# A selective-scan kernel: the scan in half blocks of channels, state sums in two column halves, the first residual on TensorE and ScalarE, and a new order of slots and transfers

## The chip, the cores and the metric

One core of one Trainium2 chip runs the whole kernel in one launch. The time is device microseconds of that core; the traces come from one profiled execution.

## The reference

For each of 64 batch entries `h` is a (205, 1024) float32 matrix: 128 rows of a token mixer (a long convolution kernel computed from `x`) and 77 rows of text. Then come a selective scan and a feed-forward layer, each on a layer norm and each added back:

```python
h = concatenate([tok(x), txt], axis=1)             # 64 x 205 x 1024
h = h + attn(layernorm(h))                         # the scan, below
h = h + ffn(layernorm(h))                          # 1024 x 1024 weights from a 4-bit table
# attn(x): dt_in (32), B (16), C (16) = x @ x_proj_w.T ; dt = softplus(dt_in @ dt_proj_w.T + b)
# per channel d (1024) and state n (16), over the 205 rows t:
#   s[t] = exp(dt[t] * A[d, n]) * s[t-1] + dt[t] * B[t, n] * x[t]
#   y[t] = sum over n of s[t] * C[t, n]   + D[d] * x[t]
```

Rows whose norm is over 64 would take 8-bit weights; a count at the end of the kernel decides that, and with these inputs none does.

## The kernel before

Three stages come first: constants, the token mixer (written to a DRAM tensor `mixed`) and the dense weights `w_low`. `scan_pass` then works through the 64 entries and takes most of the time. It is software pipelined: while entry u is scanned, entry u+1 is prepared (norm, transpose, projections, `dt`, `u = dt * x`), entry u-1 is continued (first residual `add`, second norm, first half of the feed-forward layer) and entry u-2 is ended (`ffn_late`, `out_low`, `out_high`).

**Chunks.** Channels lie on partitions: block j (0 to 7) holds 128 channels. An entry is 32 chunks; chunk s is block s//4 with four of its 16 states, 4 x 205 = 820 columns. For each chunk:

- ScalarE (ACT) writes the four decays `exp(dt * A)` into one of two PSUM buffers (L1003), once the chunk two before has been done with its buffer.
- GpSimd (POOL) writes `u * B` into a slot of `ring` with 8 slots (L1107).
- VectorE (DVE) scans (L1162) and, for the chunks in `ON_DVE` (19 of 32), multiplies by C (L1168). For the other 13 POOL multiplies by C, three chunks later (L1113).
- TensorE (PE) sums the four states, `LAG` = 3 chunks later: four float32 matmuls of the identity by 205 columns of the ring slot, accumulated in `y_ps` (L899), behind one with a diagonal of D at the start of a block (L893). After a block's last chunk ACT copies `y_ps` back into `x_t` (`blk`, L1041), and PE may start the next block.

**Order.** Each engine runs 32 slots to an entry. Slot s does the engine's part of chunk s and then what its plan (`PE_PLAN`, `ACT_PLAN`, `DVE_PLAN`, `POOL_PLAN`) lists for s. The plans are constants of the file. Everything that crosses between PE and another engine goes through two PSUM banks `xch`, in the order of `X_ORDER`, taken in turn. Entries -1 to 2 and the last three are unrolled; the others run in a hardware loop with two entries to an iteration, one such loop for each engine.

**First residual.** PE transposes `x_t` into `xch` (L915), DVE adds it to the rows in `h1` (`add`, L1183), ACT then sums the 1024 columns for the mean (`mean2`, L1019, L1022).

**Reset.** One scan instruction covers four states; `reset` (L1085) adds 1e37 to `dt` at time 0 of each block, so that the decay is 0 there.

**Transfers.** SP issues all DMAs of an entry in a fixed order and waits in it: `keep` (h1 to DRAM after the last `add`), `load` (rows of entry u+2 into `x_in`), `spread` (B and C rows to DRAM and back, broadcast over 128 partitions, into `bc`), `write` (out), `load_rows` (rows of entry u into `h1`): 10 DMAs.

Of the kernel before, what the change touches and what calls it, by code (L numbers as in the profile page):

```python
# [13 lines left out]
F32 = mybir.dt.float32  # L14
# [6 lines left out]
P = 128  # L21
# [22 lines left out]
CHUNKS = ND * NS // CN  # L44
# [18 lines left out]
def constants(nc, t, dram, kept):  # L63

    with ExitStack() as ctx:
# [10 lines left out]
        vec = sb("c_vec", [2 * ND, P])  # L76
        ps = [ctx.enter_context(nc.psum_tensor(f"c_ps{i}", [P, 512], F32)) for i in range(4)]
# [7 lines left out]
        def _(sp):  # L85
            sp.dma_start(t["a_neg"][:, :, :], dram["A_log"].rearrange("(j p) n -> p j n", p=P)).then_inc(alog_in, 16)
# [52 lines left out]
        def _(dve):  # L139
# [7 lines left out]
            for c0 in range(0, P, 32):  # L147
# [11 lines left out]
            link(dve, dve_step, n, nc.vector.tensor_scalar(  # L159
                t["a_neg"][:, :, :], t["a_neg"][:, :, :], -1.0, A_MOST, ALU.mult, ALU.min))  # L160
# [332 lines left out]
def dense_weights(nc, t, dram):  # L493
# [3 lines left out]
    with ExitStack() as ctx:  # L497
# [98 lines left out]
        def _(pe):  # L596
# [964 lines left out]
```

## Time and profile before

| | |
|---|---|
| median of 3 runs | 6199.3 us (6199.27 to 6200.41) |
| profiled execution: its own time | 6200.29 us |
| profiled execution: span of the core | 6198.4 us |
| mean granted TensorE clock | 0.979 |
| busy PE, DVE, ACT, POOL over the span | 93%, 92%, 83%, 92% |
| POOL's first instruction of scan entry 0 | at 503.63 us |

The busy shares are over all stages; the entries of the scan are read one by one, from one first POOL instruction of an entry to the next.

### The profile page before, as it was taken

Reading aid. Unit: us, or ns where it says so; the run is one execution under the profiler, and the core shown is the slowest. Engines: PE = TensorE matmul, PEld = TensorE weight load, DVE = VectorE, ACT = ScalarE, POOL = GpSimd, SP = SyncE. Lnnn points to the kernel's source line nnn. Section 1 sums busy time; section 2 is a strip of 40 time slices with the busy share of each in tenths; the row PEclk is TensorE's granted clock in tenths of the full one; section 3 lists DMA queues with packets and bytes.
Section 4 is the critical chain, followed back from the end, with each engine's and each line's share of the span. In section 5 each row is a group of like instructions: output and inputs, shape, how many; then the busy total and the mean of one; then the engine's idle time right before and its main releaser. Section 6 shows DMA issues by size and latency. Waiting matters only on the chain. (4 is left out here: it accounts for less than half of the span.)

```text
span 6198.4 us, 111922 instructions
## 1 busy us (share of the span) xinstructions
PE 5792.6 (93%) x35091; PEld 5385.1 (87%) x35091; DVE 5699.7 (92%) x4564; ACT 5122.6 (83%) x12831; POOL 5709.3 (92%) x3484
## 2 busy tenths in 40 slices
PE   4686999999999999999999999999999999999998
PEld 3555899999999999999999999999999999999997
DVE  8766999999999999999999999999999999999996
ACT  5716888888888888888888888888888888888885
POOL 4627999999999999999999999999999999999995
PEclk9887999999999999999999999999999999999999
DMA  4701222122212221222122212221222212221220
GB/s 94 161 2 66 83 88 71 67 83 88 74 64 83 88 78 66 78 88 83 61 78 88 88 56 80 86 88 61 77 83 88 72 67 83 88 78 61 83 83 34
DMA packets 115881, 478.49 MB, mean 77 GB/s; under 512 B 17441, under 2 KB 52401, under 8 KB 107122
## 3 DMA queue, kind: packets, MB, share of 16 engines
q1 hardware_dynamic: 115314, 471.10, 22.2%
q8 instruction: 335, 5.49, 0.4%
q14 instruction: 232, 1.90, 0.1%
HBM read 327.82 MB, written 143.24 MB: 76 GB/s over the span
## 5 line engine op out<-in xcount | busy, mean ns | idle before, releaser
L1107 POOL TENSOR_TENSOR s_ring<-s_bc,s_u_t 128x820 f32<-128x820 f32 x2048 | 3617.5, 1788 | 4.2 <-DMA s_bc<-rows_bc 4.2
L1003 ACT ACTIVATE s_decay<-s_dt_t,a_neg 128x205 f32<-128x205 f32 x8192 | 3047.2, 420 | 418.4 <-DVE s_ring L1168 347.5
L899 PE MATMUL s_y_ps<-s_ring,ident 128*128 128x205 f32 x16384 | 3140.6, 341 | 113.5 <-issue 61.5
L899 PEld LDWEIGHTS s_y_ps<-s_ring,ident 128*128 128x128 f32 x16384 | 2864.1, 191 | 204.9 <-POOL s_ring L1113 112.8
L1162 DVE TENSOR_TENSOR_SCAN s_decay<-s_decay,s_ring 128x820 f32<-128x820 f32 x1216 | 2265.0, 1863 | 193.6 <-ACT s_decay L1003 180.0
L1113 POOL TENSOR_TENSOR s_ring<-s_ring,s_bc 128x820 f32<-128x820 f32 x832 | 1605.4, 1930 | 77.7 <-DVE s_ring L1162 77.6
L1162 DVE TENSOR_TENSOR_SCAN s_ring<-s_decay,s_ring 128x820 f32<-128x820 f32 x832 | 1543.3, 1855 | 40.9 <-ACT s_decay L1003 40.9
L932 PE MATMUL s_xch<-s_x_t,w_low 128*128 128x205 f32 x8192 | 1523.6, 338 | 0.6 <-ACT s_x_t L1046 0.2
L932 PEld LDWEIGHTS s_xch<-s_x_t,w_low 128*128 128x128 f32 x8192 | 1422.0, 190 | 35.4 <-issue 30.6
L1168 DVE TENSOR_TENSOR s_ring<-s_decay,s_bc 128x820 f32<-128x820 f32 x1216 | 1230.2, 1012 | 41.7
L893 PE MATMUL s_y_ps<-s_x_t,s_d_diag 128*128 128x205 f32 x1024 | 279.6, 355 | 35.1 <-ACT s_x_t L1041 35.1
L1046 ACT ACTIVATE s_x_t<-s_xch 128x512 f32<-128x512 f32 (+1 forms) x512 | 244.5, 502 | 66.0 <-PE s_xch L923 64.4
L1128 POOL TENSOR_TENSOR s_u_t<-s_dt_t,s_x_t 128x410 f32<-128x410 f32 x256 | 271.7, 1061 | 18.1 <-DVE s_dt_t L1190 18.1
L1060 ACT ACTIVATE s_y_t<-s_xch,y_bias 128x205 f32<-128x205 f32 x512 | 213.7, 417 | 89.8 <-PE s_xch L932 89.8
L1041 ACT ACTIVATE s_x_t<-s_y_ps 128x205 f32<-128x205 f32 x512 | 169.6, 331 | 140.9 <-PE s_y_ps L899 140.3
L964 PE MATMUL s_p_ps<-s_xp,dtw_t 33*128 33x205 f32 x1024 | 248.2, 363 | 7.6 <-DVE s_dt_t L1190 7.1
L437 PE MATMUL t_kb<-t_mag,t_gw 128*128 128x256 f32 x512 | 138.8, 431 | 104.5 <-POOL t_gw L319 104.5
L893 PEld LDWEIGHTS s_y_ps<-s_x_t,s_d_diag 128*128 128x128 f32 x1024 | 169.7, 190 | 75.7 <-ACT s_x_t L1041 57.9
L964 PEld LDWEIGHTS s_p_ps<-s_xp,dtw_t 33*128 33x128 f32 x1024 | 166.2, 188 | 66.4 <-issue 56.9
L437 PEld LDWEIGHTS t_kb<-t_mag,t_gw 128*128 128x128 f32 x512 | 106.6, 215 | 127.1 <-POOL t_gw L319 62.6
L1197 DVE TENSOR_TENSOR s_h<-s_xch,s_h 128x512 f32<-128x512 f32 (+1 forms) x256 | 172.6, 675 | 37.6 <-PE s_xch L946 37.6
L955 PE MATMUL s_p_ps<-s_x_t,xpw_t 128*65 128x205 f32 x1024 | 200.8, 339 | 0.6 <-ACT s_x_t L1046 0.6
(165 smaller groups left out, 4224.0 us busy)
## 6 DMA issues: line engine op xcount, KB each, us to landing
s_bc<-rows_bc SPq DMA_DIRECT2D x64, 3280.0 KB, 11.0
mixed<-t_res SPq DMA_DIRECT2D x32, 1024.0 KB, 9.5
s_x_in<-mixed SPq DMA_DIRECT2D x64, 512.0 KB
s_h<-mixed SPq DMA_DIRECT2D x64, 512.0 KB
before<-s_h SPq DMA_DIRECT2D x64, 512.0 KB
out<-s_h SPq DMA_DIRECT2D x64, 512.0 KB
s_x_in<-in_txt SPq DMA_DIRECT2D x64, 308.0 KB
s_h<-in_txt SPq DMA_DIRECT2D x64, 308.0 KB
```

The costliest lines, as they stand in the source:

```text
L437: last = nc.tensor.matmul(kb[b][:, QL * k:QL * k + QL], gw[:, half, h, 2 * k:2 * k + 2, :], mag[:, half, h * QL:(h + 1) * QL], start=True, ...
L893: nc.tensor.matmul(y_ps, d_diag[:, j, :], x_t[:, par, j, :], start=True, stop=False)
L899: last = nc.tensor.matmul(y_ps, ident[:, :], ring[:, c % RING, n * LEN:(n + 1) * LEN], start=False, stop=(c % 4 == 3 and n == CN - 1))
L932: last = nc.tensor.matmul(bank[:, 0:LEN], t["w_low"][:, i, P * o:P * o + P], x2_t[:, i, :], start=(i == 0), stop=(i == ND - 1))
L964: last = nc.tensor.matmul(p_ps[:, LEN * k:LEN * k + LEN], t["dtw_t"][:, P * j:P * j + P], xp[0:RANK + 1, :], start=True, stop=True)
L1003: last = A.activation(decay[s % 2][:, n * LEN:(n + 1) * LEN], dt_t[:, par, j, :], ACT.Exp, scale=t["a_neg"][:, j, n0 + n:n0 + n + 1])
L1046: A.activation(target[:, 4 * side:4 * side + 4, cols(k)], bank[:, 0:4 * w].rearrange("p (j l) -> p j l", j=4), ACT.Copy).then_inc(empty, 1)
L1107: nc.gpsimd.tensor_tensor(ring[:, s % RING, :].rearrange("p (n l) -> p n l", n=CN), bc[:, par, n0:n0 + CN, :], u_t[:, j, :].unsqueeze(1).b ...
L1113: nc.gpsimd.tensor_tensor(ring[:, c % RING, :], ring[:, c % RING, :], bc[:, par, n0:n0 + CN, :].rearrange("p n l -> p (n l)"), ALU.mult).t ...
L1128: nc.gpsimd.tensor_tensor(u_t[:, 2 * r:2 * r + 2, :], dt_t[:, par, 2 * r:2 * r + 2, :], x_t[:, par, 2 * r:2 * r + 2, :], ALU.mult).then_in ...
L1162: V.tensor_tensor_scan(out=decay[s % 2] if s in ON_DVE else ring[:, s % RING, :], data0=decay[s % 2], data1=ring[:, s % RING, :], initial= ...
L1168: V.tensor_tensor(ring[:, s % RING, :], decay[s % 2], bc[:, par, n0:n0 + CN, :].rearrange("p n l -> p (n l)"), ALU.mult).then_inc(dve_hc, 1)
```

## The change

- **Half blocks.** A half block is 64 channels; its even states lie on partitions 0 to 63 and its odd states on 64 to 127. An entry is 16 half blocks (`NB`) x 8 states on a partition (`NK`) / 4 = 32 chunks of 820 columns, as before. `dt` and `u` are computed in the old layout (`dt_n`, `u_n`) and copied into the new one (`dt_t`, `u_t`) by DMAs within SBUF, four for each pair of blocks: 32 more DMAs an entry. `bc` holds 16 rows on a partition instead of 32 and comes in two DMAs.
- **Column-half sums.** A sum now also folds partition halves: the stationary is `stack` (two 64 x 64 identities, one above the other, 128 x 64), the output a 64-partition half of `y_ps`. Two chunks are summed together, matmul by matmul in turn: chunk c into the lower half, c+1 into the upper. The product with D becomes two matmuls of 64 columns' width. PE sums in even slots, `SUM_LAG` = 4.
- **First residual.** PE multiplies the identity by the rows in `h1` (512 columns, float32) and accumulates the transposes as ordinary matmuls on top; ACT copies the bank to `h1` and takes the row sum of each half on the way. DVE's `add` and the two long passes of `mean2` go; two short ones stand in `mean2`.
- **Reset.** Time 0 of `dt_t` is set once, and the copies leave it out; `reset` goes.
- `ON_DVE` has 20 chunks instead of 19; POOL multiplies 12.
- The plans, `X_ORDER` and the order of SP (`SP_ORDER`) are new. `load` and `load_rows` now come behind the copy of `u` for the next entry.

```diff
-CHUNKS = ND * NS // CN
+NB, NK = 2 * ND, NS // 2
+CHUNKS = NB * NK // CN
-PE_PLAN = {1: [("ffn_late", 4)], 2: [("add", 0), ("add", 1)], 6: [("add", 2), ("ffn_late", 5)], 7: [("out_low", 0)],
...
+PE_PLAN = {1: [("ffn_late", 4)], 3: [("ffn_late", 5)], 4: [("add", 0), ("out_low", 0)], 5: [("add", 1), ("add", 2)],
+           6: [("ffn_late", 6)], 7: [("add", 3)], 8: [("turn1", 0), ("ffn_late", 7)], 9: [("turn1", 1)], 10: [("turn1", 2)],
+           11: [("out_high", 0)], 13: [("turn1", 3)], 14: [("xproj", (0, 4)), ("xproj", (4, 8))], 15: [("out_high", 1)],
+           18: [("dt", 0)], 19: [("out_low", 1), ("turn2", 0), ("turn2", 1), ("dt", 1)], 20: [("turn2", 2), ("turn2", 3)],
+           22: [("ffn", 0), ("dt", 2)], 24: [("ffn", 1)], 26: [("ffn", 2)], 28: [("dt", 3)], 31: [("ffn", 3)]}
+ACT_PLAN = {0: [("mean1", 0)], 1: [("var1", 0), ("ffn_late", 4)], 2: [("blk", -1)], 3: [("ffn_late", 5), ("mean1", 1)],
+            4: [("add", 0), ("var1", 1)], 5: [("add", 1)], 6: [("norm1", 0)], 7: [("add", 2)], 8: [("blk", 0), ("ffn_late", 6)],
+            9: [("norm1", 1), ("add", 3)], 10: [("mean2", 0)], 11: [("mean2", 1), ("turn1", 0)],
...
+DVE_PLAN = {3: [("out_low", 0)], 12: [("out_high", 0)], 15: [("out_high", 1)], 18: [("out_low", 1)], 19: [("dt", 0)],
+            22: [("dt", 1)], 27: [("dt", 2)], 31: [("dt", 3)]}
+POOL_PLAN = {4: [("u_hi", 2)], 6: [("root1", 0)], 8: [("u_hi", 3)], 17: [("root2", 0)], 24: [("u_lo", 0)], 31: [("u_lo", 1)]}
+SP_ORDER = [("u_hi", 2), ("u_hi", 3), ("keep", 0), ("spread", 0), ("steps", 0), ("write", 0), ("u_lo", 0), ("load", 0),
+            ("load_rows", 0), ("steps", 1), ("steps", 2), ("u_lo", 1), ("steps", 3)]
-ON_DVE = (1, 3, 4, 5, 7, 9, 11, 13, 14, 15, 17, 19, 21, 23, 24, 25, 27, 29, 31)
+ON_DVE = (1, 3, 4, 6, 8, 9, 10, 12, 13, 14, 15, 17, 20, 21, 25, 26, 27, 29, 30, 31)
+            def halves(target, place, source, r, first, signal):
+                for i in range(2):
+                    for h in range(2):
+                        sp.dma_start(target[64 * i:64 * i + 64, place + h:place + 4:2, first:],
+                                     source[64 * h:64 * h + 64, 2 * r:2 * r + 2, first:]).then_inc(signal, 16)
+            def steps(v, par, r):
+                wait(sp, p_empty, v * P_USES + r + 2)
+                halves(dt_t, dt_place(par, 4 * r), dt_n, r, 1, dt_in[r])
+            def inputs(v, r):
+                wait(sp, u_done, v * 4 + r + 1)
+                halves(u_t, 4 * r, u_n, r, 0, u_in[r])
-                    nc.tensor.matmul(y_ps, d_diag[:, j, :], x_t[:, par, j, :], start=True, stop=False)
+                    for h in range(2):
+                        nc.tensor.matmul(y_ps[sides[h], :], d_diag[:, j, sides[h]], x_t[:, par, j, :], start=True, stop=False)
                 for n in range(CN):
-                    last = nc.tensor.matmul(y_ps, ident[:, :], ring[:, c % RING, n * LEN:(n + 1) * LEN],
-                                            start=False, stop=(c % 4 == 3 and n == CN - 1))
-                last.then_inc(sum_done, 1)
+                    for h in range(2):
+                        last = nc.tensor.matmul(y_ps[sides[h], :], t["stack"][:, :], ring[:, (c + h) % RING, n * LEN:(n + 1) * LEN],
+                                                start=False, stop=(c % 4 == 2 and n == CN - 1))
+                        if n == CN - 1:
+                            last.then_inc(sum_done, 1)
             def chunk(u, par, s, x, scan, after):
-                if s >= LAG and scan:
-                    sums(u, par, s - LAG)
+                if s % 2 != SUM_SLOT:
+                    return
+                if s >= SUM_LAG and scan:
+                    sums(u, par, s - SUM_LAG)
             def add(v, par, r, x):                                     # PE
+                nc.tensor.matmul(bank[0:rows(k), :], ident[0:rows(k), 0:rows(k)], h1[0:rows(k), par, k, 512 * side:512 * side + 512],
+                                 start=True, stop=False)
                 for j in range(4):
-                    last = nc.tensor.transpose(bank[0:rows(k), P * j:P * j + P], x_t[:, par, 4 * side + j, cols(k)], ident[:, :])
+                    last = nc.tensor.matmul(bank[0:rows(k), P * j:P * j + P], x_t[:, par, 4 * side + j, cols(k)], ident[:, :], start=False, stop=(j == 3))
+            def add(v, par, r, x):                                     # ACT
+                A.activation(h1[0:rows(k), par, k, 512 * side:512 * side + 512], bank[0:rows(k), :], ACT.Copy,
+                             accum_out=half_sum[0:rows(k), k, side:side + 1]).then_inc(empty, 1)
```

## Rows read from the trace of the kernel before

**Rows 1.** The page: busy time, share of the span and instructions of each engine.

```profile
PE 5792.6 (93%) x35091; PEld 5385.1 (87%) x35091; DVE 5699.7 (92%) x4564; ACT 5122.6 (83%) x12831; POOL 5709.3 (92%) x3484
```

**Rows 2.** Stretches: length, busy PE, PEld, DVE, ACT, POOL, clock, DMA share, GB/s.

```profile
2785.86:2872.75 86.89, 85.15 (x498) 80.10 (x497) 83.46 (x64) 76.45 (x196) 86.00 (x55) 1.00 0.21 79
2872.75:2961.28 88.53, 85.14 (x498) 80.03 (x497) 83.31 (x64) 76.47 (x196) 86.24 (x54) 1.00 0.22 78
...
3048.16:3137.99 89.83, 86.55 (x498) 81.77 (x498) 83.69 (x64) 76.62 (x196) 86.28 (x55) 0.98 0.21 77
2261.30:3137.99 876.69, 852.14 (x4944) 803.01 (x4945) 831.37 (x629) 761.91 (x1943) 857.78 (x529) 0.99 0.22 78
```

**Rows 3.** Waits in ten entries, 2257.59 to 3137.99 (total us, times, longest).

```profile
DVE s_decay L1162 <- ACT s_decay L1003: 28.2, 31, 1.8
ACT s_x_t L1041 <- PE s_y_ps L899: 21.0, 29, 1.1
...
POOL s_ring L1113 <- DVE s_ring L1162: 12.5, 21, 0.8
```

**Rows 4.** Timeline around the start of a loop iteration (start, length, engine).

```profile
3054.34 1.50 ACT L1003 ACTIVATE s_decay<-s_dt_t,a_neg 128x205 f32<-128x205 f32 x4 [2.38 <-issue]
...
3055.87 1.86 DVE L1162 TENSOR_TENSOR_SCAN s_ring<-s_decay,s_ring 128x820 f32<-128x820 f32 x1 [1.55 <-ACT s_decay L1003]
...
3060.47 2.95 PE L932 MATMUL s_xch<-s_x_t,w_low 128*128 128x205 f32 x16
```

**Rows 5.** Two stretches at that place; columns as in Rows 2.

```profile
3052.90:3056.30 3.40, 1.19 (x7) 0.88 (x6) 1.84 (x3) 1.96 (x5) 3.40 (x3) 1.00 0.01 2
3056.30:3059.70 3.40, 3.40 (x12) 3.35 (x11) 2.55 (x2) 3.34 (x10) 2.65 (x3) 0.50 0.03 5
```

**Rows 6.** Groups of instructions in ten entries, 2257.59 to 3137.99 (busy us, mean ns, idle before).

```profile
L899 PE MATMUL s_y_ps<-s_ring,ident 128*128 128x205 f32 x2560 | 490.3, 341 | 14.2 <-issue 10.8 <-POOL s_ring L1113 2.4
...
L1113 POOL TENSOR_TENSOR s_ring<-s_ring,s_bc 128x820 f32<-128x820 f32 x131 | 252.6, 1928 | 12.6 <-DVE s_ring L1162 12.5
...
L1168 DVE TENSOR_TENSOR s_ring<-s_decay,s_bc 128x820 f32<-128x820 f32 x191 | 193.2, 1012 | 6.5
...
L1046 ACT ACTIVATE s_x_t<-s_xch 128x512 f32<-128x512 f32 x40 | 23.6, 590 | 0.3
...
L1183 DVE TENSOR_TENSOR s_h<-s_xch,s_h 128x512 f32<-128x512 f32 x20 | 13.7, 683 | 0.2 <-PE s_xch L915 0.2
...
L1019 ACT ACTIVATE s_xn<-s_h 128x1024 f32<-128x1024 f32 x10 | 10.5, 1046 | 0.0
...
L1085 ACT ACTIVATE s_dt_t<-s_dt_t,s_large 128x4 f32<-128x4 f32 x20 | 5.8, 288 | 0.0
...
L1022 ACT ACTIVATE ln_in<-s_ln_sum 77x1 f32<-77x1 f32 x20 | 4.1, 203 | 0.6
...
L1019 ACT ACTIVATION_READ_ACCUMULATOR s_xn<-s_h 128x1 f32 x10 | 1.9, 191 | 0.0
```

**Rows 7.** PE's timeline in the token mixer, full and 64 x 64 stationaries in turn.

```profile
154.42 1.57 PE L437 MATMUL t_kb<-t_mag,t_gw 128*128 128x256 f32 x4 [4.42 <-POOL t_gw L319]
155.92 1.99 PE L454 MATMUL t_turned_x<-ident,t_xg 64*64 64x64 f32 x64
157.83 2.47 PE L437 MATMUL t_kb<-t_mag,t_gw 128*128 128x256 f32 x9
```

**Rows 8.** A stretch of that L454 alone (us, PE, PEld, clock, DMA share, GB/s).

```profile
156.00:157.50 1.50, 1.50 (x60) 1.50 (x64) 0.50 0.97 190
```

**Rows 9.** PE's timeline in the dense weights.

```profile
348.66 7.29 PE L607 MATMUL q_w_ps<-q_mask,q_diagonal 64*64 64x512 bf16 x132
```

**Rows 10.** SP's queue in one entry.

```profile
3027.04 0.80 SPq L824 DMA_DIRECT2D out<-s_h  x2
```

**Rows 11.** DMA issues: count, size, median us from issue to landing.

```profile
s_bc<-rows_bc SPq DMA_DIRECT2D x64, 3280.0 KB, 11.0
...
t_xg<-in_x SPq DMA_DIRECT2D x32, 128.0 KB, 9.1
```

More of the change, by code:

```diff
@@ L841, in spread @@
                 wait(sp, spread_out, v * 16 + 16)
-                sp.dma_start(bc[:, par, :, :], rows_bc[par:par + 1, :, :].broadcast_to([P, 2 * NS, LEN])).then_inc(bc_in[par], 16)
-            def entry(u, par, x, groups, ahead=True):
-                if "add" in groups:
-                    keep(u - 1, 1 - par, x)
-                if "turn1" in groups and ahead:
-                    load(u + 2, x)
-                if "turn1" in groups:
-                    spread(u + 1, 1 - par)
-                if "out_low" in groups:
-                    write(u - 2, par, x)
-                if not isinstance(u, int) or 0 <= u < BATCH:
-                    load_rows(u, par)
+                for i in range(2):
+                    sp.dma_start(bc[64 * i:64 * i + 64, par, :, :],
+                                 rows_bc[par:par + 1, i::2, :].broadcast_to([64, 2 * NK, LEN])).then_inc(bc_in[par], 16)
@@ new lines, in halves @@
+            def halves(target, place, source, r, first, signal):
+                for i in range(2):
+                    for h in range(2):
[4 more added lines that the diff above has]
+                halves(dt_t, dt_place(par, 4 * r), dt_n, r, 1, dt_in[r])
@@ new lines, in inputs @@
+            def inputs(v, r):
+                wait(sp, u_done, v * 4 + r + 1)
+                halves(u_t, 4 * r, u_n, r, 0, u_in[r])
+            def entry(u, par, x, groups, ahead=True):
+                for name, arg in SP_ORDER:
+                    if name == "keep" and "add" in groups:
+                        keep(u - 1, 1 - par, x)
+                    if name == "load" and "turn1" in groups and ahead:
+                        load(u + 2, x)
+                    if name == "spread" and "turn1" in groups:
+                        spread(u + 1, 1 - par)
+                    if name == "write" and "out_low" in groups:
+                        write(u - 2, par, x)
+                    if name == "load_rows" and (not isinstance(u, int) or 0 <= u < BATCH):
+                        load_rows(u, par)
+                    if name == "steps" and "turn1" in groups:
+                        steps(u + 1, 1 - par, arg)
+                    if name == "u_lo" and "turn1" in groups:
+                        inputs(u + 1, arg)
+                    if name == "u_hi" and (not isinstance(u, int) or 0 <= u < BATCH):
+                        inputs(u, arg)
@@ L888, in sums @@
                 j = c // 4
+                sides = [slice(64 * h, 64 * h + 64) for h in range(2)]
                 if c % 4 == 0:
@@ L1079, in soft @@
                         A.activation(d, d, ACT.Ln, bias=1.0).then_inc(soft_step, 1)
-            def reset(v, par, side):
-                wait(act, u_done, v * 4 + 2 * side + 2)
-                d = dt_t[:, par, 4 * side:4 * side + 4, 0]
-                A.activation(d, d, ACT.Identity, bias=large[:, 0, :]).then_inc(reset_done, 1)
-            stages = {"reset_lo": lambda v, par, r, x: reset(v, par, 0), "reset_hi": lambda v, par, r, x: reset(v, par, 1),
-                      "turn2": lambda v, par, r, x: turned("turn2", x2_t, r, x),
+            stages = {"add": add, "turn2": lambda v, par, r, x: turned("turn2", x2_t, r, x),
                       "turn1": lambda v, par, r, x: turned("turn1", x_t[:, par, :, :], r, x),
```

150 lines of the change are left out of this document (79 added, 71 removed), and 5 rows, old and new, of the table ACT_PLAN.

## Prediction

> **What bounds the kernel now.** I read the page first, for which engines can be the bound at all: over the whole span PE, DVE and POOL stand within a point of each other and ACT nine points lower [rows 1]. Such a share mixes stages, so the next view is single entries of the scan, cut from one first POOL instruction of an entry to the next [rows 2]. Three kinds of entry show. One takes 86.89 us, and in it POOL is busy for 86.00 us, so 0.9 us of it is idle; PE is busy for 85.15, DVE for 83.46, ACT for 76.45. The entry after it has the same work and takes 88.53; a third kind takes 89.83, with the clock at 0.98. Ten entries take 880.4 us (2257.59 to 3137.99), 88.04 each. The pace is thus POOL's, plus 1.15 us that comes from something else.
>
> The chain of waits tells how the engines hang together [rows 3]. DVE waits for ACT's decays (28.2 us in ten entries in its largest group), ACT for PE's sums (21.0), POOL for the scan (12.5). DVE has no wait for POOL of its own: a late POOL product makes a late sum, that a late `blk` on ACT, and that a late decay. So POOL's pace reaches DVE through PE and ACT, and what PE loses is felt there too.
>
> The timeline at the start of a loop iteration gives the 1.15 us [rows 4]. ACT issues nothing for 2.38 us, DVE then waits 1.55 us for its decay. PE stops as well: it is busy for 1.19 of 3.40 us while the clock is still granted in full, and in the next 3.40 us the clock is at half, 1.2 GHz, with PE busy throughout [rows 5]. An entry with a loop start costs 88.53 - 86.89 = 1.6 us more, and the fall of the clock another 89.83 - 88.53 = 1.3 us. Over two entries the first is 0.8 us an entry; the rest, 0.35, is falls.
>
> **The change part by part.** All per entry, against an undisturbed one of 86.9 us.
>
> *POOL.* It loses one of 13 products by C: 1.93 us [rows 6]. The u*B instructions keep their shape, 128x820, and `u_n` is as large as `u_t` was. POOL falls from 86.0 to 84.1, and with its present 0.9 us of idle time to an entry of 85.0.
>
> *DVE.* It loses four `add` (0.683 us for the one in the rows, the others within 0.02) and gains a product by C (1.012): -2.7 + 1.0 = -1.7 us, to 81.8 [rows 6]. If its idle time stays at 86.9 - 83.5 = 3.4 us, the entry is 85.2. That is nearly POOL's 85.0; I take 85.2. The cover is thin: POOL's gain is worth nothing beyond what DVE and ACT allow.
>
> *ACT.* Four copies of 512 columns out of PSUM come in (0.590 each, by the copy of the same size), each with a reading of the sum (0.191): +3.1. Two passes of 1024 columns with their readings go: 2 x (1.046 + 0.191) = -2.5. Two more short instructions in `mean2`: +0.4. Two `reset` go: -0.6 [rows 6]. Sum +0.5, so 77.0 of 85.2. Nothing that this engine does is on a path of its own, but all of it stands between decays, and DVE waits for those.
>
> *PE, the sums.* A float32 record of 205 columns takes (2.95 - 0.34) / 15 = 0.174 us in a steady run of 16, of which 0.34 is the length of a single one [rows 4, 6]; that is 0.85 ns a column. The 256 records of the sums are then 44.5 us. Two products into different column halves may run side by side. The trace has no 128x64 stationary, but it has 64x64 ones, in two row and two column halves. There 60 records of 64 columns pass in 1.50 us at half clock, 0.025 us each [rows 8], where 64 x 0.85 x 2 = 0.109 would be due one after the other: four at a time, float32 included. In the dense weights 132 records of 512 columns pass in 7.29 us, 0.055 each [rows 9], against 0.22 even at 0.43 ns a column. Column halves do overlap there. The bounds for the sums are 44.5 us (no overlap) and 22.3 (full); I take 22.3. The product with D keeps its 2.8 us if its two halves overlap and takes 5.6 if not.
>
> *PE, changes of the tiling.* PE goes into the half-width form and out again in up to 16 slots, 32 changes. From the full form to 64x64 in the token mixer, one row ends at 155.99 and the next starts at 155.92 [rows 7], an overlap of 0.07 (0.08 on the way back), where records in a run overlap by 0.34 - 0.17 = 0.17: about 0.1 us a change, 3.2 in all. The bounds are 0 and a whole record, 0.34, 11 in all. The Trainium skill (TensorEngine Tiling, Key Properties) says that a change of tiling mode drains the engine while independent tiles run in parallel; the row agrees with both, and a full drain at each change would only bring PE nearer to its upper bound here.
>
> *PE, the residual.* Four times two records of 512 columns at 0.85 ns are +3.5 us, and 16 transposes of one record each become two records: 16 x 0.109 = +1.7. Sum 5.2. PE in all: 85.2 - 22.2 + 3.2 + 5.2 = 71.4 us, 14 us under the entry. So PE is no bound, and its stops and the half clock have room to be caught up: of the 0.35 us of falls I leave 0.1. ACT's stop at the loop start stays, and with it 0.8 us.
>
> *Transfers.* SP issues 43 DMAs instead of 10. Two issues take 0.80 us [rows 10], so 43 are 17 us of 85. DMA share was 0.21 to 0.22 [rows 2], and the new copies are 32 x 105 KB = 3.4 MB in runs of 820 bytes against 1.6 MB that `bc` no longer brings. A copy lands, by the nearest rows, within 9.1 us (128 KB in a crowded stage) [rows 11]. The tightest user is the copy of `u` for half blocks 0 to 3. It waits for POOL's slot 24 and POOL reads it eight slots later, 8 x 2.7 = 21 us, against 2 us of issue and 9 of landing: 10 us of cover. Behind that wait in SP stand `load` and `load_rows`; they have six to eight slots until ACT's `mean1` in slot 0, and twelve until PE's `add` in slot 4. `dt` waits for DVE's slot 19 or later and is read in slot 32 or later. `write`, which stands behind the copy of `dt`, delays only `load_rows`. All at nothing; without the cover each microsecond of lateness would be a microsecond an entry.
>
> *Once.* The first entry has no cover for its copies: up to one landing, 9.1 us, between zero and that; and the constants load A twice. I take +8.
>
> **Sum.** New entry 85.2 + 0.8 + 0.1 = 86.1, against 88.04: -1.94. Sixty-two of the 64 entries run at that pace: -120. The profiled execution has a span of 6198.4 and a time of its own of 6200.3, a microsecond over the median of the runs, which I leave; 6200.3 - 120 + 8 = 6088 us.
>
> **The rivals.**
>
> *A. The pace was ACT's and DVE's chain (same or little faster).* DVE's idle time grows with what POOL gives: ACT has 0.5 us more, the chunks on DVE stand in runs of three and four, and only two decay buffers lie between. For it: all of DVE's waits are for ACT [rows 3]. Against: POOL has under 1 us idle in an undisturbed entry [rows 2]. With DVE's idle time at 4.5 to 5.2 the entry is 87.2 to 88.0: 6150 to 6205.
>
> *B. PE's late sums were behind more than the falls (faster still).* ACT's waits for PE's sums, 2.1 us an entry, and those of DVE behind them shrink, and the entry comes to POOL's 84.1 + 0.8 with hardly any idle time: 84.9, so -195: 6013.
>
> *C. The clock (slower).* PE now has 14 us idle in an entry, several slots hold nothing but a sum of 1.4 us in 5.4 us of DVE's time (slots 12, 16, 28 and 30), and the stop in rows 5 was followed by half clock. A fall that nothing covers costs 1.3 us. Two of them an entry are 2.6, more than the 1.94 saved; three give 6088 + 62 x 3.9 = 6330. It decides from 1.5 uncovered falls an entry on. Against: PE has room, and the ring lets it be a chunk or two late. The Trainium skill (TensorE: Matmul & The Clock Gate, Why this matters for your kernels) asks for matmuls kept back to back, since the clock falls when the engine pauses; rows 5 agree, and by that rule alone this rival would win.
>
> *D. The column halves do not overlap with 128 rows (much slower).* PE would be at 85.2 + 2.8 + 5.2 + 3.2 = 96.4 and the bound: with its present 1.7 us idle 98.1, +10 an entry, 6830. It decides once a record of the sums costs more than 0.087 + 14/256 = 0.14 us.
>
> *E. A copy or the rows of `x_in` come late*, by 1 to 3 us an entry: 6150 to 6275.
>
> **How the numbers follow.** Forecast (6040 to 6145) 0.50, A 0.16, B 0.12, C 0.13, D 0.03, E 0.06. The range for 8 in 10 takes the forecast, most of B (to 6005) and A and the mild end of C and E: 6005 to 6210. A measurement of this kernel tells 0.2%, 12 us, from no change. Faster by more than that (under 6187): forecast, B, three quarters of A, a third of E, 0.75. Within it: 0.07. Slower: C, D and part of E, 0.18.
>
> **What would show it.** PE busy near 71 us an entry at full clock and records of the sums every 0.09 us; POOL busy 84.1 and still the busiest; DVE at 81.8 with 3 to 4 us idle; ACT at 77; no waits of POOL or ACT for a DMA. Wrong would be: POOL idle for over 2 us an entry (A), a granted clock under 0.9 with longer waits of ACT for PE (C), PE over 85 us (D), waits for `s_u_t`, `s_dt_t` or `s_x_in` (E).

## The result and the profile after

| | before | after |
|---|---|---|
| median | 6199.29 us (6199.27 to 6200.41, 4 runs) | 6028.59 us (6026.40 to 6035.86, 4 runs) |
| ratio to before | | 0.9725 (0.9713 to 0.9736) |
| profiled execution, own time and span | 6200.29, 6198.4 us | 6035.86, 6034.1 us |
| mean granted TensorE clock | 0.979 | 0.927 |
| POOL's first instruction of scan entry 0 | 503.63 us | 508.15 us |
| ten entries, each | 88.04 us | 85.35 us |

The changed kernel is 171 us faster. The page's first line and its line on the DMA queue:

```profile
PE 5136.3 (85%) x37651; PEld 3923.5 (65%) x37651; DVE 5607.0 (93%) x4375; ACT 5087.1 (84%) x13087; POOL 5586.3 (93%) x3420
...
q1 hardware_dynamic: 535170, 578.26, 41.0%
```

PE went from 93% to 85% [rows 1]. DVE, ACT and POOL have a higher share of a shorter span. Again single entries say more. The columns are those of [rows 2]: length, busy PE, PEld, DVE, ACT, POOL, clock, DMA share, GB/s. The last row holds ten entries.

```profile
2464.65:2550.95 86.30, 75.53 (x543) 58.05 (x544) 82.63 (x61) 76.18 (x201) 84.28 (x54) 0.94 0.42 99
2550.95:2635.40 84.45, 75.06 (x534) 57.36 (x530) 81.54 (x61) 75.67 (x200) 84.16 (x53) 0.94 0.43 101
2635.40:2721.57 86.17, 75.50 (x542) 57.96 (x544) 82.56 (x61) 76.11 (x201) 84.28 (x53) 0.94 0.42 99
...
2209.45:3062.91 853.46, 753.11 (x5366) 577.07 (x5363) 820.71 (x601) 759.12 (x1992) 842.29 (x521) 0.94 0.42 100
```

Two kinds of entry are left. The short one takes 84.45 us, and POOL is busy for 84.16 of it: only 0.29 us idle. The long one, 86.2 to 86.3 us, begins with a loop start. What is new is the clock of 0.94 in *every* entry, where it was 1.00 in most entries before. Two levels, full and half, make that (1 - 0.94) x 2 x 85.35 = 10.2 us at half clock in each entry, and in these entries the trace has it in one stretch, which starts 52 to 54 us after the entry does.

The waits in the ten entries, as in [rows 3] (total us, times, longest):

```profile
PE s_xch L991 <- DVE s_h L1260: 34.8, 10, 3.5
ACT s_decay L1072 <- DVE s_ring L1239: 22.5, 45, 0.9
...
ACT s_x_t L1124 <- PE s_xch L991: 17.8, 10, 1.8
...
DVE s_ring L1233 <- ACT s_decay L1072: 13.7, 18, 1.1
...
ACT s_decay L1072 <- issue: 11.3, 5, 2.4
```

The first row is the new stop of PE: 3.5 us once an entry, until DVE has added `out_low` 1. The third is a late PE seen by ACT, once an entry. The last is ACT's stop at the loop start: five of them, 2.3 us each. No wait of ACT, POOL or DVE for a DMA stands in these entries.

TensorE alone around that stop (length, busy PE, clock, DMA share, GB/s):

```profile
2514.70:2518.10 3.40, 1.47 (x11) 0.99 0.29 89
2518.10:2521.50 3.40, 1.11 (x4) 0.50 1.11 188
...
2524.40:2527.30 2.90, 2.90 (x19) 0.50 1.17 198
```

And the timeline of the same place:

```profile
2519.00 0.66 DVE L1260 TENSOR_TENSOR s_h<-s_xch,s_h 77x512 f32<-77x512 f32 x1
...
2519.72 1.11 PE L991 MATMUL s_xch<-ident,s_xn 128*128 128x128 f32 x4 [3.54 <-DVE s_h L1260]
...
2524.36 2.95 PE L959 MATMUL s_y_ps<-s_ring,stack 128*64 128x205 f32 x16
...
2528.06 0.43 ACT L1124 ACTIVATE s_x_t<-s_xch 128x308 f32<-128x308 f32 x1 [1.78 <-PE s_xch L991]
...
2531.23 3.62 DVE L1233 TENSOR_TENSOR_SCAN s_ring<-s_decay,s_ring 128x820 f32<-128x820 f32 x2 [1.12 <-ACT s_decay L1072]
```

Read downward: PE waits 3.54 us, the clock goes from full (2.4 GHz) to half (1.2 GHz), sixteen records of the sums then take 2.95 us, ACT waits 1.78 us for PE's transposes, and DVE 1.12 us for ACT's decay. These rows show the order in time; whether one causes the next is the question of experiment 8.

At the loop start the same number of records of the sums passes at full clock, and ACT's stop stands beside them:

```profile
2465.81 1.57 PE L959 MATMUL s_y_ps<-s_ring,stack 128*64 128x205 f32 x16
...
2467.76 1.50 ACT L1072 ACTIVATE s_decay<-s_dt_t,a_neg 128x205 f32<-128x205 f32 x4 [2.33 <-issue]
...
2472.00 1.87 DVE L1233 TENSOR_TENSOR_SCAN s_decay<-s_decay,s_ring 128x820 f32<-128x820 f32 x1 [0.84 <-ACT s_decay L1072]
```

At full clock a run of 16 records now takes 1.57 us; in the full-width form it takes 2.95 [rows 4]. With 0.34 for a single record, one costs (1.57 - 0.34) / 15 = 0.082 us; it was 0.174. A record is half of a float32 matmul: the sums of an entry are 128 matmuls and stand in the trace as 256 records.

### The profile page after: what moved, and what is told of

It reads as the page before. It is cut to its first block and busy times, and to the rows that moved or that the text cites. A ratio compares the mean times of both kernels' runs of the same rounds, so it can differ in the third digit from the quotient of the medians.

```text
span 6034.1 us, 119072 instructions
## 1 busy us (share of the span) xinstructions
PE 5136.3 (85%) x37651; PEld 3923.5 (65%) x37651; DVE 5607.0 (93%) x4375; ACT 5087.1 (84%) x13087; POOL 5586.3 (93%) x3420
## 2 busy tenths in 40 slices
DMA packets 535772, 586.20 MB, mean 97 GB/s; under 512 B 52273, under 2 KB 480449, under 8 KB 535170
## 3 DMA queue, kind: packets, MB, share of 16 engines
q14 instruction: 235, 1.93, 0.1%
## 5 line engine op out<-in xcount | busy, mean ns | idle before, releaser
L959 PE MATMUL s_y_ps<-s_ring,stack 128*64 128x205 f32 x16384 | 1736.4, 356 | 57.8 <-DVE s_ring L1239 34.3
L1233 DVE TENSOR_TENSOR_SCAN s_ring<-s_decay,s_ring 128x820 f32<-128x820 f32 x768 | 1418.2, 1854 | 89.7 <-ACT s_decay L1072 84.6
L959 PEld LDWEIGHTS s_y_ps<-s_ring,stack 128*64 128x64 f32 x16384 | 1190.1, 144 | 436.8 <-issue 90.6
L951 PE MATMUL s_y_ps<-s_x_t,s_d_diag 128*64 128x205 f32 x2048 | 317.3, 391 | 118.1 <-ACT s_x_t L1119 92.5
L991 PE MATMUL s_xch<-ident,s_xn 128*128 128x128 f32 (+1 forms) x1024 | 186.9, 340 | 218.4 <-DVE s_h L1260 215.1
L983 PEld LDWEIGHTS s_xch<-ident,s_x_t 128*128 128x128 f32 (+1 forms) x2048 | 255.9, 169 | 133.8 <-issue 133.8
L991 PEld LDWEIGHTS s_xch<-ident,s_xn 128*128 128x128 f32 (+1 forms) x1024 | 139.9, 196 | 270.1 <-DVE s_h L1260 229.9
L980 PE MATMUL s_xch<-s_h,ident 128*128 128x512 f32 (+1 forms) x512 | 275.0, 618 | 32.2 <-ACT s_h L1113 32.2
L1200 POOL TENSOR_TENSOR s_u_n<-s_dt_n,s_x_t 128x410 f32<-128x410 f32 x256 | 272.5, 1065 | 17.6 <-DVE s_dt_n L1253 17.6
L983 PE MATMUL s_xch<-ident,s_x_t 128*128 128x128 f32 (+1 forms) x2048 | 267.7, 273 | 0.0
```

The source lines that it names most:

```text
L951: nc.tensor.matmul(y_ps[sides[h], :], d_diag[:, j, sides[h]], x_t[:, par, j, :], start=True, stop=False)
L959: last = nc.tensor.matmul(y_ps[sides[h], :], t["stack"][:, :], ring[:, (c + h) % RING, n * LEN:(n + 1) * LEN], start=False, stop=(c % 4 == ...
L980: nc.tensor.matmul(bank[0:rows(k), :], ident[0:rows(k), 0:rows(k)], h1[0:rows(k), par, k, 512 * side:512 * side + 512], start=True, stop=F ...
L983: last = nc.tensor.matmul(bank[0:rows(k), P * j:P * j + P], x_t[:, par, 4 * side + j, cols(k)], ident[:, :], start=False, stop=(j == 3))
L991: last = nc.tensor.transpose(bank[:, w * j:w * j + w], src[0:w, k, 512 * side + P * j:512 * side + P * j + P], ident[0:w, 0:w])
L1233: V.tensor_tensor_scan(out=decay[s % 2] if s in ON_DVE else ring[:, s % RING, :], data0=decay[s % 2], data1=ring[:, s % RING, :], initial= ...
```

## The experiments

Each ratio is to the kernel before on the same chip; each median is of 4 to 7 runs. Differences from the changed kernel's 6028.6 us are between chips: beside the experiments the kernel before took 6196.5 to 6199.8 us, beside the changed kernel 6199.3, and the changed kernel's own runs span 6026.4 to 6035.9. So a few us between two of these kernels tell nothing. Entries are told as short (no loop start) and long.

**1 and 2. One more and one less product on POOL.** Whose pace is it? Chunk 14 goes back to POOL, or chunk 23 goes to DVE as well.

```diff
-ON_DVE = (1, 3, 4, 6, 8, 9, 10, 12, 13, 14, 15, 17, 20, 21, 25, 26, 27, 29, 30, 31)
+ON_DVE = (1, 3, 4, 6, 8, 9, 10, 12, 13, 15, 17, 20, 21, 25, 26, 27, 29, 30, 31)              # 1
+ON_DVE = (1, 3, 4, 6, 8, 9, 10, 12, 13, 14, 15, 17, 20, 21, 23, 25, 26, 27, 29, 30, 31)      # 2
```

> The changed kernel with one product by C (chunk 14) given back from VectorE to GpSimd: 19 and 13. If GpSimd sets the pace, each of 64 entries takes one more product of 1.93 us: an entry without a loop start 86.4 us, the kernel 6028.6 + 124 = 6152 us. If the chain of VectorE and ScalarE sets it, VectorE has 1.01 us less to do and the kernel takes 5965 to 6029 us.

> The changed kernel with one more product by C (chunk 23) on VectorE: 21 and 11. If GpSimd alone sets the pace, 1.93 us an entry less, 5905 us. If VectorE with its 2.9 us of idle time is level with it, as I forecast (81.5 + 1.0 + 2.9 = 85.4 an entry), 6090 us. If VectorE's idle time is slack that only waits for GpSimd's pace, its busy time of 82.6 plus some 1.5 us is the floor: 84.1, 6010 us.

Measured: 6098.46 us, ratio 0.9839 (0.9823 to 0.9856), and 6035.06, 0.974 (0.9724 to 0.9756). With 19 chunks on DVE, two entries in turn, the second with a loop start:

```profile
2576.18:2662.36 86.18, 74.82 (x536) 57.24 (x534) 81.44 (x60) 76.19 (x199) 86.02 (x54) 0.94 0.43 99
2662.36:2748.54 86.18, 76.27 (x536) 58.38 (x534) 80.61 (x59) 75.53 (x199) 86.02 (x54) 0.92 0.42 99
```

With 21:

```profile
2545.94:2630.84 84.90, 74.98 (x538) 57.49 (x537) 82.69 (x62) 76.28 (x200) 82.44 (x52) 0.94 0.43 100
2630.84:2716.70 85.86, 74.97 (x538) 57.45 (x537) 82.90 (x62) 76.14 (x200) 82.56 (x52) 0.94 0.43 100
```

The first pair settles the short entry: POOL gets 1.86 us more work, the short entry gets 86.18 - 84.45 = 1.73 longer, and POOL is busy in all but 0.16 us. POOL sets it. It also shows what the long entry is: it took 86.2 us in the changed kernel too, with POOL at 84.3, so POOL does not set the pace there but the ACT and DVE chain (with a late PE in it, by experiment 8), and under a POOL of 86.0 us the loop start is covered. That is why the +70 us lie between the two numbers expected, which had the loop start added on top. The second pair takes 1.7 us from POOL and the short entry does not follow; it *grows* to 84.90, of which DVE is busy for 82.69. So POOL at 84.2 and the ACT and DVE chain at some 84 stand side by side. 20 chunks is the balance: 19 cost 70 us, and 21 bring nothing, since 6035.1 us is the changed kernel's time within its runs.

**3. The order of the sums' matmuls.** The same eight matmuls (16 records) of a pair of chunks, four into the lower half first and then four into the upper, instead of in turn.

```diff
-                for n in range(CN):
-                    for h in range(2):
+                for h in range(2):
+                    for n in range(CN):
```

> The eight matmuls of a pair of chunks in another order: four into the lower half of the columns, then four into the upper, instead of one and one in turn. If two column halves run side by side only when they alternate, the sums take 44 us an entry instead of 22, TensorE is at 97 us and the bound, and the kernel takes 6700 to 6850 us. If TensorE can also pass four waiting matmuls to reach the other half, or if the overlap is not what shortened the sums, the time stays within 1% of 6029 us.

Measured: 6433.38 us, 1.0383 (1.0366 to 1.04). A run of sums in its timeline:

```profile
2702.79 2.31 PE L959 MATMUL s_y_ps<-s_ring,stack 128*64 128x205 f32 x16
```

And an entry:

```profile
2687.55:2779.05 91.50, 86.06 (x539) 67.51 (x536) 81.86 (x60) 76.26 (x200) 84.37 (x53) 0.94 0.39 93
```

A record costs (2.31 - 0.34) / 15 = 0.131 us. With four matmuls of one half behind each other the halves overlap only in part, so the time lies between the two that were expected. PE is busy for 86.1 us, 11 more than in the changed kernel and more than any other engine. It is still idle for 5.4 us; the others wait for it in this entry (ACT 4.7 us in all for the feed-forward products, DVE 3.4 us once for transposes). The full overlap needs the alternating order; the half-width form alone does not give it.

**4. The residual back on DVE.** In the changed kernel PE only transposes, DVE adds in slots 3, 4, 5 and 7, and `mean2` has its two long passes again. The plans are otherwise those of the change.

```diff
-                nc.tensor.matmul(bank[0:rows(k), :], ident[0:rows(k), 0:rows(k)], h1[0:rows(k), par, k, 512 * side:512 * side + 512],
-                                 start=True, stop=False)
...
-DVE_PLAN = {3: [("out_low", 0)],
+DVE_PLAN = {3: [("add", 0), ("out_low", 0)], 4: [("add", 1)], 5: [("add", 2)], 7: [("add", 3)],
```

> The changed kernel with the first residual as it was: TensorE transposes only, VectorE adds (slots 3, 4, 5 and 7), ScalarE sums 1024 columns in two long passes. VectorE has 2.7 us more (84.2 us an entry), ScalarE 0.5 less, TensorE 5.2 less. If VectorE's idle time of 2.9 us stays as it is, an entry takes 87.1 us and the kernel 6200. If it is slack, VectorE's 84.2 is just level with GpSimd's 84.2 and the entry takes about 85: 6065 us.

Measured: 6177.92 us, 0.997 (0.9957 to 0.9982). An entry:

```profile
2606.49:2693.56 87.07, 72.00 (x506) 55.36 (x502) 84.12 (x65) 75.16 (x192) 84.05 (x53) 0.90 0.41 98
```

PE has 15 us of room and POOL 3.0 us; DVE is busy for 84.12 and idle for 2.95, as much as in the changed kernel. That speaks for DVE's load as what sets the entry, and 6177.9 - 6028.6 = 149 of the 171 us hang on taking the additions from it. It is not shown apart from the plan, which was not made anew for this kernel: in this entry PE waits 3.5 us for ACT's copy of a block and POOL 2.9 us for PE's sum, each once, and the clock is at 0.90 instead of 0.94. So 149 is an upper bound of what the residual is worth.

**5. The product alone.** The kernel before, with chunk 28 on DVE as the twentieth.

```diff
-ON_DVE = (1, 3, 4, 5, 7, 9, 11, 13, 14, 15, 17, 19, 21, 23, 24, 25, 27, 29, 31)
+ON_DVE = (1, 3, 4, 5, 7, 9, 11, 13, 14, 15, 17, 19, 21, 23, 24, 25, 27, 28, 29, 31)
```

> The kernel before with one product by C (chunk 28) moved from GpSimd to VectorE, 20 and 12, and nothing else. If GpSimd alone sets the pace, 6199 - 64 x 1.9 = 6077 us. If VectorE is as near, as the two runs with 19 and 21 products in the changed kernel say, it has 84.5 us of work here and with 3.0 us idle takes 87.5 an entry: 6200 to 6235 us, no gain or a loss.

Measured: 6221.1 us, 1.0032 (1.0021 to 1.0044).

```profile
2609.94:2697.05 87.11, 84.87 (x498) 80.10 (x496) 84.11 (x65) 76.41 (x196) 84.11 (x54) 1.00 0.22 78
```

POOL is down to 84.11 and nothing is gained: DVE is up to 84.11 and keeps 3.0 us of idle time, as in experiment 4. Against the 6198.2 us of the kernel before on this chip it costs 23 us. A short entry is only 0.2 us longer; two entries with a loop start take 90.2 and 90.3 us, where [rows 2] have 88.5 and 89.8.

Experiment 4 has the same 20 products and DVE's `add` too, but half blocks, column halves and the new order: 6221.1 - 6177.9 = 43 us is what those bring together. No run takes them apart.

**6. The residual alone.** The kernel before with experiment 5's chunk and the residual on PE and ACT, in whole blocks. The edits are the reverse of those of experiment 4, in `add`, `mean2`, `ACT_PLAN` (slots 3, 4, 6, 8) and `DVE_PLAN`.

```diff
-DVE_PLAN = {3: [("add", 0)], 4: [("add", 1)], 6: [("add", 2)], 7: [("out_low", 0)], 8: [("add", 3)], 16: [("out_low", 1)],
+DVE_PLAN = {7: [("out_low", 0)], 16: [("out_low", 1)],
```

> The kernel before with the residual of the changed one (rows of h1 and transposes accumulated by TensorE, copied and summed by ScalarE, no add on VectorE) and 20 products by C on VectorE, but whole blocks, full-width sums and the old plan. GpSimd and VectorE then have the 84.1 and 81.8 us of the changed kernel, TensorE 85.2 + 5.2 = 90.4. If TensorE's time is why the column halves are needed, an entry takes 90.4 to 92 us and the kernel 6350 to 6450. If GpSimd and VectorE decide and the ring covers TensorE, it takes about 6080.

Measured: 6565.75 us, 1.059 (1.0572 to 1.0608). A short entry:

```profile
2734.43:2826.72 92.29, 89.72 (x521) 83.32 (x520) 82.13 (x61) 76.83 (x202) 84.23 (x54) 1.00 0.20 74
```

Its waits in ten entries:

```profile
DVE s_decay L1178 <- ACT s_decay L1009: 104.1, 65, 4.1
...
ACT s_h L1051 <- PE s_xch L921: 53.7, 30, 2.5
```

The direction was expected, the size (6350 to 6450) was not. PE is busy for 89.7 us. On top ACT stands before its copies until PE is done with the 512-column products and the transposes, and DVE waits behind ACT's decays. The residual costs 6565.8 - 6221.1 = 345 us over experiment 5 here, and with column halves and the new plan it brings up to 149. This plan was made for DVE's `add`; how much of the 345 is PE's load and how much the old order was not run.

**7. Twice as many copies.** Each of the 32 copies within SBUF becomes two of one block each. The bytes are the same.

```diff
-                        sp.dma_start(target[64 * i:64 * i + 64, place + h:place + 4:2, first:],
-                                     source[64 * h:64 * h + 64, 2 * r:2 * r + 2, first:]).then_inc(signal, 16)
+                        for k in range(2):
+                            sp.dma_start(target[64 * i:64 * i + 64, place + h + 2 * k, first:],
+                                         source[64 * h:64 * h + 64, 2 * r + k, first:]).then_inc(signal, 16)
```

> The changed kernel with each copy of dt and u cut into two DMAs of one column block, so 64 copies an entry instead of 32, with the same bytes and runs. If the copies have cover, as the forecast has it, SP is busy for some 30 to 45 of 85 us and the time stays at 6029 us, within 10. If SP's queue is close to its limit, GpSimd or ScalarE wait for s_u_t, s_dt_t or s_x_in and the time goes up by 30 us or more.

Measured: 6032.3 us, 0.9733 (0.9718 to 0.9748). SP's queue, one step of `u`:

```profile
2551.00 5.67 SPq L879 DMA_DIRECT2D s_u_t<-s_u_n  x8
```

The same in the changed kernel:

```profile
2464.72 3.29 SPq L878 DMA_DIRECT2D s_u_t<-s_u_n  x4
```

Another 2.4 us at this step (2.4 to 3.3 at the others of the entry that have no wait in them) reached nobody: the time is the same, and the transfers are covered.

**8. Filling PE's stop.** Eight float32 matmuls of 205 columns go between `out_low` 1 and `turn2`, into columns of `y_ps`'s bank that nothing reads. The rest of the kernel is as it was.

```diff
-           ... 19: [("out_low", 1), ("turn2", 0), ("turn2", 1), ("dt", 1)],
+           ... 19: [("out_low", 1), ("fill", 8), ("turn2", 0), ("turn2", 1), ("dt", 1)],
+            def fill(v, par, n, x):
+                for _ in range(n):
+                    nc.tensor.matmul(spare, ident[:, :], t["w_low"][:, 0, 0:LEN], start=True, stop=True)
```

> The changed kernel with eight matmuls of 205 columns, whose result nobody reads, in TensorE's slot 19, where it stands still for 3.5 us of each entry before the clock falls to half for 10.2 us. The granted clock should go from 0.93 to 0.98 or more. If the falls cost nothing because TensorE has room, 6025 to 6035 us. If they are what an entry with a loop start loses, or make TensorE's sums late for GpSimd, 5980 to 6010 us.

Measured: 5990.17 us, 0.9668 (0.9652 to 0.9684), 38 us less than the changed kernel. A short and a long entry:

```profile
2534.72:2618.93 84.21, 74.12 (x548) 57.52 (x546) 81.65 (x61) 75.88 (x199) 84.05 (x54) 1.00 0.42 101
2618.93:2703.59 84.66, 77.48 (x554) 60.08 (x552) 81.15 (x60) 75.33 (x198) 84.24 (x54) 0.96 0.43 101
```

PE's wait for `out_low` 1 falls from 34.8 to 7.0 us in ten entries, ACT's for the transposes behind it from 17.8 to 9.6, and DVE's behind ACT from 13.7 to 7.2. The clock is only half mended: its mean is 0.960, where 0.98 was expected. The first entry stays at full clock; most others still have 3.4 or 6.8 us at half, about 56 us into the entry, instead of 10.2.

The short entry gains only 0.2 us, since POOL sets it; the long one comes from 86.2 to 84.7. So the clock's price is paid in the entries with a loop start. The 29 long entries in the loop show it in one trace, with the filling the same in all of them. Six follow a short entry whose fall lasts for 6.8 us in one piece, from 55 to 62 us: they take 85.8 to 85.9. The other 23 follow one with no fall or with falls of 3.4 us each: they take 84.3 to 84.7, hardly more than a short one. So a long fall late in an entry and the loop start that comes next cost little apart and some 1.5 us together.

**9. Fewer loop starts.** Four entries to an iteration instead of two, so 15 starts instead of 30.

```diff
-            with engine.Fori(0, (BATCH - 4) // 2) as i:
-                entry(i * 2 + 3, 1, Exchange(i * (2 * X_STEP) + x_start(3)), X_GROUPS)
-                entry(i * 2 + 4, 0, Exchange(i * (2 * X_STEP) + x_start(4)), X_GROUPS)
+            with engine.Fori(0, (BATCH - 4) // 4) as i:
+                for k in range(4):
+                    entry(i * 4 + 3 + k, 1 - k % 2, Exchange(i * (4 * X_STEP) + x_start(3 + k)), X_GROUPS)
```

> The changed kernel with four entries to an iteration of the engines' loops instead of two (SP's keeps two), so 15 loop starts instead of 30. In the changed kernel an entry with a loop start takes 86.2 us and one without 84.4. If the start is what costs the 1.8 us, 15 x 1.8 = 27 us go: 6002 us. If it is something with a period of two entries, such as the buffers that alternate, the time stays at 6029; if fetching the longer code costs more, it is above.

Measured: 6004.13 us, 0.9687 (0.967 to 0.9703): 24.5 us less for 15 starts, 1.6 us each. SP's loop keeps two entries. The long entries again go with the clock: with 6.8 us at half in themselves and in the entry before they take 85.0 to 85.5 us, with 10.2 in both 86.5 to 86.7.

**10. The stop made shorter.** DVE ends `out_low` 1 one slot earlier.

```diff
-DVE_PLAN = {... 15: [("out_high", 1)], 18: [("out_low", 1)], 19: [("dt", 0)],
+DVE_PLAN = {... 15: [("out_high", 1)], 17: [("out_low", 1)], 19: [("dt", 0)],
```

> The changed kernel with the second out_low on VectorE in slot 17 instead of 18, nothing added. TensorE stands still for it for 3.5 us of each entry and the clock falls behind that. A slot of VectorE is 2.7 us, so the stop shrinks to about 1 us. If the stop and the half clock behind it were what the eight spare matmuls took away, the granted clock rises to 0.95 or more and the time comes to 5985 to 6000 us. If the spare matmuls worked in another way, by holding TensorE back, the time stays near 6029.

Measured: 6031.34 us, 0.973 (0.9717 to 0.9743), no gain. Its largest wait of PE in ten entries:

```profile
PE s_p_ps L1032 <- DVE s_dt_n L1253: 32.0, 10, 3.3
```

The stop at `turn2` was halved, to 1.7 us an entry, and a stop of 3.2 us at the next step, the `dt` projection, took its place. The mean clock stayed at 0.929, where 0.95 had been expected, so this run does not test what a kernel without the fall would take. Shortening a stop by moving one producer only handed it on; filling it with work did not.

**11. Both at once.** Experiment 8's matmuls and experiment 9's loop.

> The eight spare matmuls and the loop of four entries together. Alone they brought 38 and 25 us. If both act on the same reserve, that of the chain of ScalarE and VectorE in an entry with a loop start, there is little left for the second: 84.2 to 84.3 us in every entry, 5975 to 5985 us. If they act on separate costs, 6029 - 38 - 25 = 5966 us.

Measured: 5992.49 us, 0.9671 (0.9658 to 0.9685). Alone the two gave 38 and 24.5 us; together 36, a smaller gain than either expectation had (times of 5975 to 5985, or 5966). They are the same microseconds: the chain can absorb ACT's stop or a slow PE, and not both close together. With the filling alone a long entry is on average only 0.4 us over a short one (84.77 and 84.33), so there was little left for fewer starts to save. With both, a long entry is 0.8 us over a short one (85.13 and 84.38), and there are half as many.

**12. The fill and 21 products on DVE.**

> The spare matmuls together with 21 products by C on VectorE. With 21 products and the falls of the clock, GpSimd has 82.4 us of work and an entry without a loop start takes 84.9 us, at the pace of ScalarE and VectorE. In the trace of the changed kernel, ScalarE waits 1.8 us for the transposes that TensorE makes at half clock, and VectorE then 1.1 us for a decay. If that wait is on the pace-setting chain, an entry comes down by up to 1.1 us to 83.8 and the kernel to 5965 us, the fastest here. If it has slack elsewhere, the entry without a loop start stays at 84.9 and the kernel at 6000 to 6035.

Measured: 5980.56 us (5973.28 to 5984.06), 0.9646 (0.9633 to 0.9659), the fastest kernel of the study. Two entries:

```profile
2532.60:2616.68 84.08, 76.93 (x559) 60.01 (x558) 82.93 (x62) 76.63 (x202) 82.37 (x52) 0.98 0.43 101
2616.68:2701.59 84.91, 76.24 (x555) 59.39 (x554) 83.01 (x62) 76.25 (x200) 82.48 (x52) 0.98 0.44 101
```

With PE on time DVE runs with 1.2 to 1.9 us of idle time, so the product that brought nothing in experiment 2 now brings 10 us: the runs with 20 products lie at 5986 to 5999 us, these at 5973 to 5984. The gain is smaller than the 1.7 us an entry that POOL was given, as the chain takes over at some 84, and the time lies between the two expected. With POOL out of the way a long fall shows in the short entries too. Those in the loop take 83.7 to 83.8 us without a fall, 83.3 to 84.1 with 3.4 us at half, 83.9 to 84.9 with 6.8, and in experiment 2, with 10.2 in each, 84.9.

## Why the prediction was right, and where its sizes were off

6088 was forecast, with 6005 to 6210, and 6028.6 was measured. The mechanism held in the main: POOL and DVE get lighter, PE gets room, the transfers are covered. The entry gained 2.69 us where 1.94 was forecast. Two terms held in number and not in what they are made of, the loop start and the part paid once.

**POOL, held.** 84.1 forecast, 84.16 measured. Its price for a product did not move, though DMA share doubled and the clock fell more often; from the groups of the ten entries:

```profile
L1185 POOL TENSOR_TENSOR s_ring<-s_ring,s_bc 128x820 f32<-128x820 f32 x120 | 231.7, 1931 | 0.6
```

**DVE's busy time, held; its idle time, mis-sized.** 81.8 forecast, 81.54 measured. The step "if its idle time stays at 3.4 us, the entry is 85.2" was the term that was off: the idle time is 84.45 - 81.54 = 2.9 us. POOL's was taken over as 0.9 and is 0.29, so POOL sets the short entry. Experiments 1 and 2 put the two bounds within half a microsecond: 84.2 for POOL, and for the chain 84.9 with 21 products, less one product, 83.9. The miss of 0.75 us an entry is as large as this term's, 85.2 against 84.45.

**ACT, held.** 77.0 forecast, 75.7 to 76.2 measured. Its copy out of PSUM, where 0.590 us was taken:

```profile
L1113 ACT ACTIVATE s_h<-s_xch 128x512 f32<-128x512 f32 x20 | 11.5, 574 | 0.0
```

**PE's sums, held (rival D is out).** Full overlap was taken, 0.087 us a record; it is 0.082. Experiment 3 adds what the prediction did not say, that it needs the alternating order. By the Trainium skill (TensorEngine Tiling, Key Properties) different tiles can execute their matmuls in parallel. The 0.082 us agrees, and experiment 3's 0.131 is a case in which it holds only in part. PE in all is 75.06 us against 71.4; 10.2 us of each entry pass at half clock, in which 2.95 us are taken for what needs 1.57, so a few of these 3.7 us are the clock's. What a change of the tiling costs was not measured by itself; the forecast's 3.2 us compares an overlap at half clock [rows 7, 8] with one at full clock.

**Loop starts, held in number, in part by luck.** 0.8 us an entry was forecast, for ACT's stop alone. A long entry is 1.7 to 1.9 us over a short one, 0.9 an entry; experiment 9 gives 1.6 a start. But behind an entry with no long fall the stop costs hardly anything (84.3 to 84.7 us in experiment 8). What is paid is the stop and the fall before it together.

**Falls of the clock: rival C's cause came, its price did not.** The forecast had them at 0.1 us. Now every entry has 10.2 us at half clock, not only slots without work as rival C had it, but behind one wait for DVE. (Of the four slots that it names, slot 28 has a `dt` step in `PE_PLAN`.) Rival C priced an uncovered fall at 1.3 us, from [rows 2]. In a short entry the price is 0.2 us, since POOL sets it, and up to 1.2 once POOL is lighter (84.9 in experiment 2, 83.7 without a fall in experiment 12); in a long one it is joined to ACT's stop. Filling the stop brings 38 us, 0.6 an entry. So the 0.1 was too low, and it did not show in the sum because the stop's 0.8 already stood there. The Trainium skill (TensorE: Matmul & The Clock Gate, Why this matters for your kernels) asks that TensorE be not left idle for long between bursts of matmuls. The 0.50 behind the 3.54 us wait agrees; what it costs is told by the experiments.

**Rivals A, B and E.** A asked for 4.5 us of idle time on DVE; it has 2.9. B is nearer to the result than the forecast is, in the average entry (84.9, against 85.35 measured) and in the time (6013): POOL has hardly any idle time left, and the largest group of DVE's waits for ACT fell from 28.2 [rows 3] to 13.7 us. B's own sign came in full: ACT's wait for PE's sums, 21.0 us in ten entries [rows 3], is gone.

```profile
L1119 ACT ACTIVATE s_x_t<-s_y_ps 128x205 f32<-128x205 f32 x80 | 25.8, 323 | 0.0
```

Experiment 3 has the same order with slower sums, and there this wait is 5.7 us. So a good part of it went with the new order and `SUM_LAG`, and not only with the faster sums. What kept the result from B's number is the long entry. C's number for one fall, 1.3 us, is near what a fall costs a long entry here (1.5), and far from what it costs a short one. E is out in the steady state: the copies land fast, and experiment 7 puts more load on SP without a loss.

```profile
s_bc<-rows_bc SPq DMA_DIRECT2D x128, 820.0 KB, 8.6
s_u_t<-s_u_n SPq DMA_DIRECT2D x1024, 102.5 KB, 2.3
s_dt_t<-s_dt_n SPq DMA_DIRECT2D x1024, 102.0 KB, 4.8
```

SP's price was too low, 0.40 us an issue against 3.29 / 4 = 0.82 and 5.67 / 8 = 0.71 in the rows of experiment 7, and 2.56 / 4 = 0.64 in other steps; it lay under cover.

**Once, held in number, in part by luck.** +8 was forecast, for copies without cover in the first entry and constants that load twice. The scan starts 508.15 - 503.63 = 4.5 us later, and from the end of POOL's last `u * B` to the end of the kernel it takes 79.2 us instead of 75.5, which the forecast did not name: +8.2. The start moves from run to run as well: in the traces of experiments 1, 2 and 10, with the same code up to there, it is at 508.0, 504.6 and 506.3 us. The late start is a copy without cover, in the timeline of entry 0:

```profile
508.15 6.97 POOL L1179 TENSOR_TENSOR s_ring<-s_bc,s_u_t 128x820 f32<-128x820 f32 x4 [8.08 <-DMA s_u_t<-s_u_n]
```

**The sum.** Over all 64 entries, up to the end of the last `u * B`, the mean is 85.105 us against 87.801: 64 x -2.696 = -172.5, and +8.2 makes 6200.3 - 164.3 = 6036, the profiled execution. It is the slowest of the four; their median is 7 us lower.

**Left open.** What holds ACT for 2.3 us at a loop start is shown by no view (it stands as "issue"). Experiments 4 and 6 with plans made for them, and the new order of slots by itself, were not tried. That the length of a long entry goes with the fall before it is read from how the entries of single traces differ; no run moved the fall alone.

## What to carry to other kernels

Where several engines stand within a few per cent of each other, moving work off one of them is worth nothing, or less, until the one that receives it has room: here the product alone cost 23 us, the residual on top of it, without column halves and in the old plan, 345 more, and with the column halves, the residual and the product together the kernel gained 171. An engine's idle time in an undisturbed entry is a term of its own, and not a fixed one: DVE's was 2.9 to 3.4 us in the kernel before, the changed one and experiments 4 and 5, 2.2 in experiment 2 and 1.2 once PE was on time. Test which engine is on top by moving one unit of work each way. A stop of TensorE that is harmless alone can meet another stall soon after it; see whether useful or spare matmuls in it pay before reordering its producer.

## What the runs showed of the hardware

- Two half-width float32 products over 128 rows overlap fully when their matmuls alternate between the column halves (0.082 us a record of 205 columns, two records to a matmul, against 0.174 at full width), and only in part when four matmuls of one half follow each other (0.131).
- One wait of 3.5 us in an entry was followed by 10.2 us at half clock, where PE was busy without a gap for part of it (2.90 of 2.90 us at 0.50). With eight spare matmuls in the wait it was 0 to 6.8 us in most entries.
- 535,772 DMA packets instead of 115,881 and a DMA share of 0.42 instead of 0.22 left POOL's instruction of 820 columns at 1.93 us and DVE's at 1.01.
